# Differential attention plus gated MLP on one core: the scores move from bfloat16 stacks to float32 matmuls over four row groups

## The reference, cut to what matters

```python
# x: 8 x 256 tokens x 256; H = 16 heads of 16, q has 32 heads, two for each k/v head
q = concat(heads(x @ Wq1), heads(x @ Wq2)); k = heads(x @ Wk); v = heads(x @ Wv)
p = softmax(causal(q @ k.T / 4))
y = p @ v
y = y[:16] - sigmoid(x @ Wlam) * y[16:]
x = layernorm(x + y @ Wo)
gate: silu(x @ sh_gate.T) * (x @ sh_up.T) @ sh_down.T            # 1024 wide
routed: the same, 128 wide, times the sum of the softmax of the top 2 of 8 router logits
x = layernorm(x + shared + routed)
```

## Time and profile before

| | before |
|---|---|
| median of 3 runs | 476.25 us (476.05 to 477.08) |
| the profiled execution, its own time | 476.44 us |
| its span, first to last instruction | 474.7 us |
| PE busy | 422.8 us (89%) |
| DVE / POOL / ACT busy | 279.8 / 244.1 / 235.7 us |
| moved by DMA | 40.41 MB |

### The profile page before, as it was taken

The page is one execution under the profiler, slowest core; times in us unless marked ns, Lnnn a source line. Parts: engine busy times, 40 slices in busy tenths (PEclk is TensorE's granted clock), DMA queues, the critical chain, the costliest instruction groups (busy, mean ns, idle before and its releaser), DMA issues.

```text
span 474.7 us, 10336 instructions
## 1 busy us (share of the span) xinstructions
PE 422.8 (89%) x4008; PEld 340.2 (72%) x4008; DVE 279.8 (59%) x676; ACT 235.7 (50%) x532; POOL 244.1 (51%) x334
## 2 busy tenths in 40 slices
PE   4238697899999999999999999999999999997995
PEld 4126146795799668975898669975898579856995
DVE  3637136763568547663768366745867478746374
ACT  4604481538444763568244843577265832583240
POOL 8305373617355663658355845667355831483142
PEclk9859697979999999999999999999999999999899
DMA  8762760246003800353113710371024410000000
GB/s 284 243 150 76 200 172 2 79 115 155 1 25 100 201 25 23 91 149 90 46 54 98 174 46 14 111 180 43 28 79 115 112 46 1 4 1 24 1 23 23
DMA packets 34753, 40.41 MB, mean 85 GB/s; under 512 B 4240, under 2 KB 28304, under 8 KB 34448
## 3 DMA queue, kind: packets, MB, share of 16 engines
q1 hardware_dynamic: 34704, 39.75, 30.8%
HBM read 27.94 MB, written 11.53 MB: 83 GB/s over the span
## 4 chain that ended last, share of the span: by engine, by line
PE 69%; ACT 13%; DVE 9%; DMA 3%; issue 2%; SPq 2%; POOL 1%; POOLq 0%; DVEq 0%; ACTq 0%
PE ff L668 10%; PE ff L670 9%; PE ff L669 9%; PE ybank L780 8%; ACT prob L514 8%; PE ring L731 7%; PE ybank L668 4%; PE ring L726 4%; PE ring L752 3%; PE ybank L670 3%; PE ybank L669 3%; PE ring L756 3%; DVE neg_max L1013 2%; ACT gate_t L522 2%; ACT h_hi L474 2%
## 5 line engine op out<-in xcount | busy, mean ns | idle before, releaser
L1013 DVE TENSOR_REDUCE neg_max<-ring 128x2 f32<-128x512 f32 (+3 forms) x176 | 102.6, 638 | 39.3 <-PE ring L731 38.7
L514 ACT ACTIVATE prob<-ring 128x512 f32<-128x512 f32 x192 | 100.3, 621 | 14.9 <-PE ring L752 14.8
L399 POOL TENSOR_TENSOR h_lo<-h_full,h_hi 128x256 fp32r<-128x256 f32 x72 | 52.9, 734 | 102.5 <-ACT h_hi L474 102.5
L409 POOL TENSOR_SCALAR_AFFINE_SELECT prob<-prob 128x512 f32<-128x512 f32 x128 | 83.3, 675 | 24.1 <-ACT prob L514 23.7
L668 PE MATMUL ff<-x1T_hi,wg_lo 128*128 128x256 f32 x288 | 87.3, 303 | 0.1
L669 PE MATMUL ff<-x1T_lo,wg_hi 128*128 128x256 f32 x288 | 81.2, 282 | 0.0
L670 PE MATMUL ff<-x1T_hi,wg_hi 128*128 128x256 f32 x288 | 81.1, 282 | 0.0
L1034 DVE COPY yv<-ybank 128x256 f32<-128x256 f32 x64 | 26.5, 422 | 75.6 <-PE ybank L780 75.6
L726 PE MATMUL ring<-mask_b,ident_b 128*128 128x128 bf16 (+2 forms) x176 | 45.3, 258 | 19.2 <-DMA q_stack<-qk_parts_dram 17.3
L731 PE MATMUL ring<-k_stack,q_stack 96*128 96x256 bf16 (+3 forms) x512 | 60.7, 239 | 0.0
L668 PEld LDWEIGHTS ff<-x1T_hi,wg_lo 128*128 128x128 f32 x288 | 55.1, 191 | 3.4 <-issue 1.3
(11 more groups left out here) (164 smaller groups left out, 912.3 us busy)
## 6 DMA issues: line engine op xcount, KB each, us to landing
q_stack<-qk_parts_dram SPq DMA_DIRECT2D x48, 256.0 KB, 4.5
qk_parts_dram<-parts SPq DMA_DIRECT2D x72, 128.0 KB
k_stack<-qk_parts_dram SPq DMA_DIRECT2D x48, 128.0 KB, 4.3
xt_raw<-xT SPq DMA_DIRECT2D x8, 256.0 KB, 2.8
xz<-x SPq DMA_DIRECT2D x8, 256.0 KB, 2.8
out<-xz SPq DMA_DIRECT2D x7, 256.0 KB, 2.2
prob<-w_gu SPq DMA_DIRECT2D x1, 1152.0 KB, 7.2
yv<-w_gu SPq DMA_DIRECT2D x1, 1024.0 KB, 8.8
```

Source lines behind the costliest of these rows:

```text
L399: pool.tensor_tensor(h_lo[:, n, :], h_full[:, n % RING, :], h_hi[:, n, :].bitcast(F32), ALU.subtract).then_inc(h_lo_done, 1)
L409: pool.affine_select(out=v, in_=v, compare_op=ALU.is_ge, fill=0.0, base=0, pattern=[[0, 2], [HALF, 2], [0, 2], [1, HALF]], channel_multipl ...
L514: act.activation(prob[:, g % RING, u, :], ring[u][:, :], ACT.Exp, scale=SCALE).then_inc(exp_done, 1)
L1013: dve.tensor_reduce(neg_max[:, columns.start:columns.stop, i], ring[u % RING][:, 0:len(columns) * keys].rearrange("p (h k) -> p h k", k=keys),
```

## The change

The stacks, their three-part split and the DRAM scratch go. ACT writes q and k out of PSUM as float32, twice each (`query_rows`, `key_rows`): a 32-partition row group holds two heads of 16 rows, and a column of ones and zeros (`parity`) keeps one head in each copy; the freed rows of the k copy are ones in one place (`other_row`), so that the maxima, loaded as one float32 row, are subtracted in the matmul. A score matmul contracts over 32 rows, and four of them, one for each row group, stand next to each other in the program and write four different banks (three ring banks and `misc`). The 22 maxima tiles become six `quad`s of four banks, the eight probability groups six `t_round`s of four banks; the other work is put between these. The transposes leave `misc` for `ybank[1]`. The gate and up weights are now split before the first iteration by ACT and POOL, through the banks of `prob`.

```diff
-S_TILE_HEADS = (8, 4, 2, 2)
+QUADS = ((0, 0, 2), (1, 0, 2), (2, 0, 1), (2, 1, 2), (3, 0, 1), (3, 1, 2))
+T_ROUNDS = ((0, 0), (0, 4), (0, 8), (1, 0), (1, 4), (1, 8))
-QK_AT = (3, 6, 10)
-X1T_AT, ROUTER_AT, LOGIT_AT = 11, 15, 19
-SHARED_AT, ROUTED_AT = (1, 5, 8, 12), 18
-FF_FIRST, FF_MAX, FF_Y0, FF_Y1 = 0, range(1, 4), 7, 8
-FF_SCORES = {0: 4, 2: 5, 4: 6}
+QK_AT = (1, 3, 5)
+X1T_AT, ROUTER_AT, LOGIT_AT = 2, 3, 5
+SHARED_AT, ROUTED_AT = (0, 1, 2, 4), 4
+FF_FIRST, FF_MAX, FF_Y0, FF_Y1 = 0, range(1, 3), 7, 8
+FF_ROUNDS = {0: 3, 1: 4, 2: 5, 5: 6}
+H_ROUNDS = {0: 2, 1: 3, 2: 4, 3: 5}
+PV_ROUNDS = {3: (0, 1), 4: (2, 3), 5: (4, 5, 6, 7)}
...
+        q_rows = [sb(f"q_rows{k}", [P, PARITIES, Q_JOBS, 2 * T]) for k in range(STACKS)]
+        k_rows = [sb(f"k_rows{k}", [P, PARITIES, KEY_BLOCKS, T]) for k in range(STACKS)]
...
+            def query_rows(b, n):
...
+                for x in range(PARITIES):
+                    act.activation(query_order(q_rows[b % STACKS][:, x, n, :]), psum_order(qk_bank(b, n)[:, :]), ACT.Copy,
+                                   scale=parity[:, x:x + 1]).then_inc(q_done, 1)
+            def key_rows(b):
+                act.wait_ge(qk_full, (b + 1) * QK_JOBS)
+                for x in range(PARITIES):
+                    act.activation(k_rows[b % STACKS][:, x, :, :], qk_bank(b, QK_JOBS - 1)[:, :].rearrange("p (n t) -> p n t", n=KEY_BLOCKS),
+                                   ACT.Identity, bias=other_row[:, x:x + 1], scale=parity[:, x:x + 1]).then_inc(k_done, 1)
...
+            def quad(b, q):
...
+                for u in units:
+                    if q > 0:
+                        pe.wait_ge(max_done, b * S_UNITS + u - ROW_GROUPS + 1)
...
+                for j, (x, block) in enumerate(tiles):
+                    for row in range(ROW_GROUPS):
+                        rows = slice(row * ROW_GROUP, (row + 1) * ROW_GROUP)
+                        mm = pe.matmul(score_banks[row][:, j * keys:(j + 1) * keys], q_rows[b % STACKS][rows, x, block, i * P:(i + 1) * P],
+                                       k_rows[b % STACKS][rows, x, block, 0:keys], start=False, stop=True, skip_group_check=True)
...
+            def t_round(b, k):
...
+                        if half == 0 and k == 0:
+                            pe.wait_ge(max_loaded, (b + 1) * (16 * PARITIES))
+                        elif half == 0:
+                            pe.wait_ge(exp_done, b * T_UNITS + (k - 1) * ROW_GROUPS + j + 1)
...
+                for k in range(len(T_ROUNDS)):
+                    t_round(i, k)
+                    if has_prev and k in FF_ROUNDS:
+                        gu_units(i - 1, (FF_ROUNDS[k],))
+                    for g in PV_ROUNDS.get(k, ()):
+                        pv_group(i, g, has_next)
```

More of the change, by code:

```diff
@@ L222, in is_first, with spot, query_order, s_tile @@
             return b == 0
[L224 to L233, removed]
+        def spot(n):
+            group, row = divmod(n, ROW_GROUPS)
+            block, x = divmod(group, PARITIES)
+            return slice(row * ROW_GROUP, (row + 1) * ROW_GROUP), x, block
         def psum_order(ap):
             return ap.rearrange("p (h i t) -> p h i t", h=2, i=Q_TILES)
[L238 to L240 removed]
+        def query_order(ap):
+            return ap.rearrange("p (i h t) -> p h i t", h=2, i=Q_TILES)
+        def s_tile(u):
+            i, first, end = QUADS[u // ROW_GROUPS]
+            return i, u % ROW_GROUPS, range(first, end), (i + 1) * HALF
+        def causal_count(b, w, u):
+            return b * len(CAUSAL_ORDER) + CAUSAL_ORDER.index((w, u)) + 1
+        def prob_of(w, u):
+            return prob[:, PROB_AT[w][u], :]
+        def exp_count(b, w, u):
+            return b * T_UNITS + T_ORDER.index((w, u)) + 1
         def qk_bank(b, n):
[L243 removed]
+            return (ybank[0], ybank[1], misc)[n] if is_first(b) else ybank[0]
+        def v_bank(b, t):
+            return ff[t] if is_first(b) else ring[1 + t]
         block = ctx.enter_context(nc.Block())
@@ L509, in exps @@
-            def exps(b, g, units=range(3)):
-                for u in units:
-                    act.wait_ge(t_full, b * T_UNITS + 3 * g + u + 1)
-                    if u == 0 and g >= RING:
-                        act.wait_ge(pv_full, b * GROUPS + g - RING + 1)
-                    act.activation(prob[:, g % RING, u, :], ring[u][:, :], ACT.Exp, scale=SCALE).then_inc(exp_done, 1)
+                    act.wait_ge(max_loaded, b * (16 * PARITIES))
+                copy(max_rows[:, :], misc[0:MAX_ROWS, 0:P]).then_inc(max_copied, 1)
@@ new lines, in exps @@
+            def exps(b, k):
+                w, first = T_ROUNDS[k]
+                if is_first(b) and k in (1, 3):
+                    act.wait_ge(mlp_w_lo_done, 1 + k // 3)
+                for j in range(ROW_GROUPS):
+                    act.wait_ge(t_full, exp_count(b, w, first + j))
+                    if j == 0 and k >= 4:
+                        act.wait_ge(pv_full, b * GROUPS + 2 * (k - 3))
+                    act.activation(prob_of(w, first + j), score_banks[j][:, :], ACT.Exp, scale=SCALE).then_inc(exp_done, 1)
@@ new lines, in t_round @@
+            def t_round(b, k):
+                w, first = T_ROUNDS[k]
+                halves = range(2) if first == CORNERS else range(1)
+                for half in halves:
+                    for j in range(ROW_GROUPS):
+                        if half == 0 and k == 0:
+                            pe.wait_ge(max_loaded, (b + 1) * (16 * PARITIES))
+                        elif half == 0:
+                            pe.wait_ge(exp_done, b * T_UNITS + (k - 1) * ROW_GROUPS + j + 1)
+                        if first == CORNERS:
+                            rows, x, block = spot((2 * w + half) * ROW_GROUPS + j)
+                            o, keys, tokens = score_banks[j][:, half * T:(half + 1) * T], slice(P, T), slice(T, 2 * T)
+                        else:
+                            rows, x, block = spot(2 * w * ROW_GROUPS + first + j)
+                            o, keys, tokens = score_banks[j][:, :], slice(0, P), slice(0, 2 * T)
+                        mm = pe.matmul(o, k_rows[b % STACKS][rows, x, block, keys], q_rows[b % STACKS][rows, x, block, tokens], start=True, stop=True)
+                        if half == halves[-1]:
+                            mm.then_inc(t_full, 1)
@@ L944, in iteration @@
                 if has_next:
[L945 to L946 removed]
+                    quad(i + 1, 0)
                 wo_job(i)
```

550 lines of the change are left out of this document (216 added, 334 removed).

## The result

| | before | after |
|---|---|---|
| median | 476.3 us (476.05 to 477.08, 4 runs) | 520.32 us (515.24 to 523.36, 4 runs) |
| ratio to before | | 1.0836 (1.0794 to 1.0879) |
| the profiled execution, its span | 476.44, 474.7 us | 517.32, 515.3 us |
| PE busy | 422.8 us (89%) | 470.4 us (91%) |

The kernel became 8.4% slower: the way that was forecast, but by 40 us where 18.6 were forecast.

The account below looks back on a forecast made before the run. PE's own time was taken to bound the seven later iterations, a DMA of the q stack the start. 476.4 - 11.7 (start) + 2.8 (second) + 20.5 (five middle) + 7.0 (last) = 495.0 us; 8-in-10 range 465 to 525.

Parts of the forecast that it names:

- first mask: Start: the first quad waits only for two ACT key-bank copies, so it comes at 13.9 instead of 31.61 us, -17.7.
- first maxima: First entry's maxima: DVE's 12.6 us and six quads in turn make 20.7 us, against 17.20 before, +3.5.
- start in all: Start of the run: earlier first quad less slower first maxima and probabilities, -11.7 us, bounds -14.2 to -8.
- steady: maxima: Maxima of a steady iteration: columns 0.5, switches 0.6 and waits for banks DVE still reads 0.8, +1.9 us.
- steady: load and probabilities: Steady iteration: +0.5 us waiting for the loaded maxima, +1.4 for probability rounds waiting on exponentials, 21.0 us by the order.
- last, with the end: Last entry, no next projections between quads: maxima 20.4 us against 15.60, +4.8; with 1.4, 0.5 and 0.3, +7.0 (3 to 9).
- End of an iteration: +0.3: End of an iteration: a moved value product covers PE's 0.6 us wait, a quad adds 0.6, the output product waits some 0.3.
- Six rounds of 3.2: First iteration's probabilities: six rounds of 3.2 us with nothing to cover them make 19.2 us, against 16.70 before, +2.5.
- The price of a column: Float32 score matmuls: 0.93 to 1.03 ns per column pass, read off the strips; +0.5 us in maxima, +1.0 in probabilities.
- Rival C: Score matmuls: row groups don't run side by side at all, +31 us an iteration, about 730 us; chance 0.05.
- rival B: Score matmuls: a set's four weight loads run one after the other, +10 us in each of eight, about 565; chance 0.10.
- Rival A: Whole kernel faster: row groups interleave, ACT and DVE hidden behind PE, +0.7 us an iteration, about 469.6 us; chance 0.25.

Follow-up runs that it names:

- first run: Against the changed kernel, only ACT's order differs: the second value bank's copy stands ahead of the last unit's gate; 491.87 us, ratio 1.0332.
- run with the filler: Changed kernel plus 16 mask matmuls into a free bank ahead of the first quad of each next entry; 506.87 us, ratio 1.064.
- fifth run: Values first plus, in the first iteration, 26 mask matmuls ahead of the first round and 13 after each of four rounds; 488.54 us, ratio 1.0246.
- half the exponentials: Values first, float32 rows, with exponentials of 256 of 512 columns of each bank from the second entry on; 478.95 us, ratio 1.0034.
- runs with one pass: Values first with q and k copies and maxima row in one-pass formats: bfloat16 447.05 us, ratio 0.9374; float32r 452.48 us, ratio 0.9477.

## Why the prediction was too low

Its steps, beside what the trace after shows (stage lengths from the rows and windows above; the second, seventh and last entries from the same view):

| term | forecast | measured |
|---|---|---|
| first mask | -17.7 | -17.1 (14.52 for 31.61) |
| first maxima | +3.5 | +5.5 (22.63 for 17.17) |
| first probabilities | +2.5 | +7.9 (24.21 for 16.35) |
| start in all | -11.7 | -5.4 (second entry at 72.25 for 77.62; load and end of the first make the other -1.6) |
| steady: maxima | +1.9 | +2.1 at the full clock, +3.6 to +5.2 behind a fall |
| steady: load and probabilities | +1.9 | +1.5 (23.92 for 22.46) |
| steady: end of an iteration | +0.3 | +1.3 (8.96 for 7.62) |
| five middle iterations | +20.5 | +32.2 |
| second iteration | +2.8 | +3.7 |
| last, with the end | +7.0 | +10.1 |
| sum | +18.6 | +40.6 of the span |

**The step that failed first** is "End of an iteration: +0.3". I went through what the moved product covers and did not ask which banks the first quad needs. It needs all four, two of them are the value banks, and ACT empties those last. I had read ACT's order only at the start. The first run, values first, shows this step's price: with the copy moved, the end of an iteration is 6.87 us, 0.75 less than before, and the whole kernel takes 491.9 us, near the 495 forecast. That it comes so near is partly chance. By the profile of that run the start is worth -9.3 us where -11.7 was forecast (second entry at 68.36), and a steady iteration grows by 3.0 where 4.1 was forecast.

**The second** is that I gave no term to the clock in the steady iterations. The granted clock of before is 1.00 in its middle, so I took it as given. It is not: behind six of the seven waits PE's products stand about 0.22 us apart instead of 0.12, the lower of the two levels, for some 3.5 us in four entries and some 7 us in two. The run with the filler prices this at 9.3 us by itself.

**The third** is the first probabilities. "Six rounds of 3.2" assumed that ACT paces them; at a clock of 0.68 PE was busy 22.07 of the 24.21 us and ACT 12.39. The fifth run brings the clock to 1.00 and gets 20.47 us, filler and all, where 19.2 were forecast. The first maxima were sized too small: PE waits for DVE there (0.93 us at 37.15 is the last of those waits). A part of this miss is the clock again. The first mask comes at 14.52 us here and at 13.37 in the first run, because PE's first projection products stand 0.21 us apart until 11.7 us here and only until 9.0 there; the first maxima then take 22.63 us at a granted clock of 0.92 here and 21.45 at 1.00 there. No edit touches these stages, and no run tells what decides between the two.

The last entry was read from the wrong place. From its first mask its maxima took 17.72 us before (390.01 to 407.73), not the 15.60 from 392.1 that the sum held. They take 25.83 after, at a granted clock of 0.87, and 22.9 in the first run: 5.2 more than before, so that the +4.8 comes close there is chance.

**What held.** The price of a column: two sets of four matmuls of the quads, and a round of probabilities with the product behind it, in the timeline after (they answer to the earlier trace rows):

```profile
263.41 0.39 PE L684 MATMUL ring<-k_rows,q_rows 32*128 32x256 f32 x3
...
263.62 0.39 PE L684 MATMUL ring<-k_rows,q_rows 32*128 32x256 f32 x3
...
274.25 0.70 PE L709 MATMUL ring<-q_rows,k_rows 32*128 32x512 f32 x3
...
274.78 0.60 PE L709 MATMUL ring<-q_rows,k_rows 32*128 32x512 f32 x3
...
275.32 0.39 PE L626 MATMUL ff<-x1T_hi,wg_lo 128*128 128x256 f32 x1
```

Four matmuls of 256 columns take 0.21 us for a pass, four of 512 take 0.53: 0.82 and 1.04 ns per column, near what was read off the strips. Rival C is out, and so is rival B: a set of four loads would take 0.43 us, a whole pass of 256 columns takes half of that. (Rival B's 565 does not follow from its own terms: 10 us in each of eight iterations on top of 495 make 575. Nothing rests on it.) The Trainium skill, "TensorEngine Tiling (Array Packing)", section Key Properties, says that different tiles can load weights and multiply in parallel; the trace agrees with these 0.21 us.

The float32 passes of an iteration add up to 10.7 us: four rounds of 1.06, two of 0.86, and in the quads eight passes of 0.11 twice, four of 0.165 twice and four of 0.21 twice. The prediction had 10.5 to 11.6. In the run with bfloat16 rows, two sets of four matmuls of 256 columns stand 0.12 us apart, no more than one product of 256 columns takes there (four of 512 take 0.32 us with the switch behind them, 235.86 to 236.18):

```profile
229.36 0.28 PE L685 MATMUL ring<-k_rows,q_rows 32*128 32x256 bf16 x3
...
229.48 0.28 PE L685 MATMUL ring<-k_rows,q_rows 32*128 32x256 bf16 x3
```

An estimate by another page of the Trainium skill, "TensorE: Matmul & The Clock Gate", section Measured speedup vs the span model, was 13.7 us of score matmuls and a sum of 520. The trace does not show that loss, so that the measured time lies near this 520 is chance. It is luck, too, that it lies inside the range of 465 to 525: neither of its bounds had a wait for ACT's copy or a fall of the clock in it.

The probabilities came out at 20.69 us where the prediction's walk through the order gave 21.0, and half the exponentials show that its reason, rounds waiting for the last bank, was right. The DMA of the maxima was not waited for in the steady iterations: PE is busy for all of the 3.23 us. Of the waits that were to be seen in the profile after, PE's for DVE stand in the first two entries and the last only, and the one for the maxima's DMA in the first; from 128.82 on the middle has none but that for the values. The maxima of the middle have no wait for DVE, so their +2.1 us are columns, masks and switches and not the 0.8 of waiting that the sum held; that only the total of this term fits is chance. Rival A was to win below 1.7 us an iteration; even with the wait gone the growth is 3.0 (54.9 for 51.9): +2.3 in the maxima, +1.5 in load and probabilities, -0.75 at the end. The runs with one pass take it away: the same row groups then need 50.05 and 49.3 us, less than the 51.9 of before. The lasting price of this change was the second pass of float32, not the row groups.

## What to carry to other kernels

When a change takes more banks at once, ask for each of them who reads it last and where that reader's instruction stands in its own engine's order; here one copy that came too late cost some 22 us, the lower clock behind the wait included, and moving it is free. A wait on a busy PE can cost more than its length, as the clock fell behind six of the seven here: price it with the rows at both clocks, and test it by filling the wait with useless work. The transfers that were hidden in the steady state here were worth only their share of the start, and the four row groups paid once each matmul was one pass.

## What had not been expected of the hardware

A float32 pass of four row groups takes 0.11 us with 64 columns and with 128 alike, so quads of 64 keys are no cheaper than those of 128; with bfloat16 rows the two take 0.03 and 0.06 us. A float32 pass of 512 columns takes 0.53 us, more than twice the 0.21 of 256; no run tells why. In the first iteration the clock fell while PE was working in rounds of 32-row matmuls with short waits between them, and stayed at 1.00 when 128-row matmuls stood in those places, though they computed nothing that is used.
